# A transformer block on one core: the closing sums are dealt to VectorE, TensorE and GpSimd by a table, two parts more are read ahead, and the reads begin at another signal

## The chip, the cores and the metric

One core of a Trainium2 chip runs the whole program. The metric is the time on the device in microseconds (us), the median of several executions. Engines are called PE or TensorE (matmuls), DVE or VectorE, ACT or ScalarE, POOL or GpSimd; SP only issues DMAs.

## The reference, cut to what matters

The input is 64 sequences of 64 tokens of 256 floats (4096 tokens). A conditioned down/up projection, attention and a routed feed-forward layer follow. The end of it is what the change touches: each token goes to 4 of 32 experts, and their weighted outputs are added to the token's residual and to the input.

```python
topv, topi = jax.lax.top_k(glogits, TOPK)            # TOPK = 4 of E = 32
gw = jax.nn.softmax(topv, axis=-1)
combine = jnp.zeros((N, E), x.dtype).at[jnp.arange(N)[:, None], topi].add(gw)
def body(acc, we):
    wu, wd, ce = we
    u, g = (h2 @ wu)[:, :DFF], (h2 @ wu)[:, DFF:]
    return acc + ce[:, None] * (jax.nn.silu(g) * u @ wd), None
y2, _ = jax.lax.scan(body, jnp.zeros_like(h2), (W_up, W_down, combine.T))
return x + y2.reshape(Bx, Tx, Dx)                    # and the caller: x = x + this
```

## The kernel before

The first part (to about 575 us) computes attention and routing and writes each token's row into lists in DRAM, one list for each expert. The second part, the expert loop, walks over `NET` = 161 tiles of 128 list rows. The number is the worst case; how many tiles hold rows is known only at run time, and here 142 do (the last 19 are empty and are computed all the same). For each tile ACT starts the load of its rows (`rows_in`, six tiles ahead), PE turns and multiplies them with the expert's weights, which lie in a ring of four slots, DVE and ACT do the elementwise work, ACT writes the result to `rows_out` (`NY` = 6 buffers), and POOL scatters it by an indirect DMA to `pick_rows` in DRAM, where the four results of a token lie side by side (`s_put`, six semaphores, one for each buffer, count the landings). Every twelve tiles DVE also adds input rows into `resid`, which holds the residual of all tokens in SBUF.

The end follows the loop in each engine's program. `PARTS` = 8 parts of `NP` = 4 token tiles are read back from `pick_rows`, 2 MB each (`picks`: for a tile of 128 tokens, 4 rows of 256 floats on each partition). SP issues the reads into `NPICK` = 5 buffers: part 5 goes into the buffer of part 0 and so on, so it waits until part 0's sums are done. SP issues the first read when `s_rows_out` has reached the number of filled tiles plus 6; the tile that brings it there could only be written after the last filled tile's scatter had landed, because it uses the same buffer.

Of each part DVE sums three tiles in three instructions: first the four rows of each tile to two, then the two to one, then into `resid`. PE sums the fourth by matmuls with the identity into PSUM (one for `resid`, four for the picks), and ACT copies that from PSUM into `resid` and issues the tile's store. Ahead of its first copy ACT waits for the last six scatters to land. SP stores DVE's three tiles of each part, after it has issued all reads.

Each engine runs its own program in order; the order of the first part stands in hand-written tables and is not touched.

Of the kernel before, what the change touches and what calls it, by code (L numbers as in the profile page):

```python
# [23 lines left out]
E, TOPK, DFF = 32, 4, 256  # L24
# [7 lines left out]
NT = NTOK // P  # L32
# [16 lines left out]
WE = KC * 2 * DFF + FC * D  # L49
# [5 lines left out]
NW, NU, NPAY, NG, NY, NC = 5, 3, 3, 10, 6, 4  # L55
# [4 lines left out]

NP = 4
PARTS = NT // NP
NPICK = 5
BATCH = 8

NX, XSTEP = 4, 12

# [152 lines left out]
def program(nc, d):  # L220
# [30 lines left out]
    def sb1(name, shape, dt=F32):  # L251
# [175 lines left out]
    s_sum, s_summed = sem("s_sum"), sem("s_summed")  # L427
    s_act_upper, s_up_upper, s_up_split = sem("s_act_upper"), sem("s_up_upper"), sem("s_up_split")


# [48 lines left out]
    def sync_program(e):  # L479
# [108 lines left out]
        w.wait_ge(s_ug, 1)  # L588
        for k in range(2 * TPM):
            w.wait_ge(s_x2_row[(LAST - k) % (2 * TPM)], 16 * ((LAST - k) // (2 * TPM) + 1))  # L590
        e.dma_start(resid[:, :, :], x2_rows.rearrange("(t p) n -> p t n", p=P)).then_inc(s_back, 16)
        w.wait_ge(s_ring_wait, 1)
        for n in range(RING, E):
# [4 lines left out]

        w.wait_ge(s_resid, NT // NX)
# [9 lines left out]
        for c in range(PARTS):  # L611
            w.wait_ge(s_final, c + 1)
            e.dma_start(d["out"][c * NP * P:(c * NP + NP - 1) * P, :].rearrange("(t p) n -> p t n", p=P),
                        resid[:, c * NP:c * NP + NP - 1, :]).then_inc(s_out, 16)
        w.wait_ge(s_out, 16 * 2 * PARTS)

    def gpsimd_program(e):
# [78 lines left out]

        for i in range(NET):
            scatter(i)  # L700

    def tensor_program(e):
# [317 lines left out]


        w.wait_ge(s_mid, NET)
        for c in range(PARTS):
            bank, t = gbank[c % 2][:, 0:D], c * NP + NP - 1
            if c >= 2:
                w.wait_ge(s_summed, c - 1)
            w.wait_ge(s_resid, NT // NX)
            e.matmul(bank, ident[:, :], resid[:, t, :], start=True, stop=False)  # L1030
            w.wait_ge(s_picks[c % NPICK], 16 * (c // NPICK + 1))
            for k in range(TOPK):
                ins = e.matmul(bank, ident[:, :], picks[c % NPICK][:, NP - 1, k, :], start=False, stop=k == TOPK - 1)
            ins.then_inc(s_sum, 1)

    def scalar_program(e):
# [244 lines left out]
        for c in range(PARTS):  # L1283
            t = c * NP + NP - 1
            w.wait_ge(s_sum, c + 1)
            e.activation(resid[:, t, :], gbank[c % 2][:, 0:D], ACT.Copy).then_inc(s_summed, 1)
            w.wait_ge(s_summed, c + 1)
            e.dma_start(d["out"][t * P:(t + 1) * P, :], resid[:, t, :]).then_inc(s_out, 16)

    def vector_program(e):
# [334 lines left out]
        e.tensor_scalar(all_out[:, :], ends[0:1, E - 1:E], float(AHEAD + NY), None, ALU.add)  # L1627
# [24 lines left out]
        def turn_mid(i):  # L1652
# [15 lines left out]
        for i in range(NET + 2):  # L1668
            if i >= 2:
                turn_mid(i - 2)  # L1670
            if 0 < i < NET - 2:
                turn_in(i + 2)
            if i < NET:
                expert_mid(i)
            if i == 0:
                turn_in(2)
            if i % XSTEP == 0 and 3 <= i // XSTEP < 3 + NT // NX:
                residual(i // XSTEP - 3)

        for c in range(PARTS):  # L1680
            pk = picks[c % NPICK]
            w.wait_ge(s_picks[c % NPICK], 16 * (c // NPICK + 1))
            at = slice(c * NP, c * NP + NP - 1)
            half = own.mark(e.tensor_tensor(pk[:, 0:NP - 1, 0:2, :], pk[:, 0:NP - 1, 0:2, :], pk[:, 0:NP - 1, 2:4, :], ALU.add))
            w.wait_ge(s_vector, half)
            whole = own.mark(e.tensor_tensor(pk[:, 0:NP - 1, 0, :], pk[:, 0:NP - 1, 0, :], pk[:, 0:NP - 1, 1, :], ALU.add))
            w.wait_ge(s_back, 16)
            w.wait_ge(s_vector, whole)
            e.tensor_tensor(resid[:, at, :], resid[:, at, :], pk[:, 0:NP - 1, 0, :], ALU.add).then_inc(s_final, 1)

    banks_for = banks_of()
    with ctx:
# [23 lines left out]
def _constants():  # L1716

    f = np.float32
    p = np.arange(P)
    pos = np.arange(T, dtype=f) / f(32.0)  # L1720
    inv = (f(1.0) / np.power(f(150000.0), np.arange(0, DH, 2, dtype=f) / f(DH))).astype(f)
    angle = (pos[:, None] * inv[None, :]).astype(f)
    cos, sin = np.cos(angle).T[p % 32], np.sin(angle).T[p % 32]
    scale = f(DH ** -0.5)

    unused = np.zeros((P, ROW), f)
    unused[:, D] = PAIRS + p
# [19 lines left out]


# [48 lines left out]
```

## Time and profile before

| what | value |
|---|---|
| median of 3 runs | 1031.28 us (1029.86 to 1033.35) |
| profiled execution, first to last instruction (its span) | 1031.5 us |
| busy share of the span: PE, DVE, ACT, POOL | 87%, 78%, 50%, 54% |
| bytes moved by DMA | 251.95 MB, mean 244 GB/s |

The profiled execution is one execution; the record gives its span, and no other time of it, and the span is 0.2 us above the median of the runs. Times in the trace are counted from the span's start. Busy shares are means over stages that have different limits, so the end must be read by itself. The loop's last DVE instruction ends at 996 us, and everything after that is the end.

### The profile page before, as it was taken

Reading aid. Unit: us, or ns where it says so; the run is one execution under the profiler, and the core shown is the slowest. Engines: PE = TensorE matmul, PEld = TensorE weight load, DVE = VectorE, ACT = ScalarE, POOL = GpSimd, SP = SyncE. Lnnn points to the kernel's source line nnn. Section 1 sums busy time; section 2 is a strip of 40 time slices with the busy share of each in tenths; the row PEclk is TensorE's granted clock in tenths of the full one; section 3 lists DMA queues with packets and bytes.
Section 4 is the critical chain, followed back from the end, with each engine's and each line's share of the span. In section 5 each row is a group of like instructions: output and inputs, shape, how many; then the busy total and the mean of one; then the engine's idle time right before and its main releaser. Section 6 shows DMA issues by size and latency. Waiting matters only on the chain.

```text
span 1031.5 us, 21542 instructions
## 1 busy us (share of the span) xinstructions
PE 898.5 (87%) x7336; PEld 738.7 (72%) x7336; DVE 805.3 (78%) x1877; ACT 512.2 (50%) x1193; POOL 552.1 (54%) x513
## 2 busy tenths in 40 slices
PE   3859998988899989988871399999999999999986
PEld 1537676776677767766750288888888888888874
DVE  3878799988978898988857177777777777777787
ACT  1224362735437363453752266666666666566631
POOL 2436466877768688696768133333433344333340
PEclk9869999999999999999995599999999999999998
DMA  7235869687696977959875897778678758663599
GB/s 224 57 93 181 268 218 268 224 275 250 232 290 214 295 241 252 293 192 301 289 252 202 325 307 266 264 243 309 224 254 273 265 186 308 223 226 103 179 365 340
DMA packets 127684, 251.95 MB, mean 244 GB/s; under 512 B 18706, under 2 KB 66327, under 8 KB 127002
## 3 DMA queue, kind: packets, MB, share of 16 engines
q1 hardware_dynamic: 83866, 187.59, 55.4%
q0 software_dynamic: 13872, 34.64, 9.2%
q10 hardware_dynamic: 29840, 28.34, 9.0%
q8 instruction: 63, 1.03, 0.4%
q14 instruction: 43, 0.35, 0.1%
HBM read 136.19 MB, written 102.66 MB: 232 GB/s over the span
## 4 chain that ended last, share of the span: by engine, by line
PE 49%; POOL 14%; DMA 11%; DVE 10%; issue 7%; SPq 4%; ACT 3%; ACTq 0%; DVEq 0%; POOLq 0%
PE scores L970 10%; PE gbank L970 10%; POOL lists L672 10%; PE scores L989 5%; PE gbank L989 5%; DMA w_parts<-ring 4%; PE gbank L761 3%; DMA ring<-in_W_up 3%; POOL ring L679 3%; PE gbank L838 3%; DMA rows_in<-lists 3%; DVE ring L1401 2%; PE gbank L944 2%; PE scores L944 2%; PE gbank L979 2%
## 5 line engine op out<-in xcount | busy, mean ns | idle before, releaser
L694 POOL DMA_INDIRECT pick_rows<-rows_out,pair_i x161 | 160.9, 999 | 269.4 <-ACT rows_out L1232 260.7
L679 POOL TENSOR_TENSOR ring<-ring 128x512 fp32r<-128x512 f32 x96 | 122.6, 1291 | 47.0 <-ACT ring L1167 46.5
L970 PE MATMUL scores<-ring,in_part 128*128 x486 | 134.7, 412 | 0.0
L970 PE MATMUL gbank<-ring,in_part 128*128 x480 | 131.8, 409 | 0.0
L672 POOL DMA_INDIRECT lists<-put_rows,slot_i x104 | 103.4, 994 | 47.5 <-issue 28.0
L838 PE MATMUL gbank<-w_o,ring 128*128 128x256 f32 x512 | 123.2, 396 | 6.0 <-ACT ring L1113 6.0
L761 PE MATMUL gbank<-h_t,w_qk 128*128 128x512 f32 x480 | 122.1, 407 | 6.7 <-DVE h_t L1388 5.0
L1401 DVE SCALAR_TENSOR_TENSOR ring<-gbank,b_qk,rope 128x512 f32<-128x512 f32 x160 | 109.9, 745 | 16.6 <-PE gbank L761 16.0
L838 PEld LDWEIGHTS gbank<-w_o,ring 128*128 128x128 f32 x512 | 99.8, 199 | 26.0 <-ACT ring L1113 9.7
L761 PEld LDWEIGHTS gbank<-h_t,w_qk 128*128 128x128 f32 x480 | 89.7, 192 | 31.5 <-issue 8.6
L1167 ACT ACTIVATE ring<-ring 128x512 fp32r<-128x512 f32 x96 | 59.9, 628 | 90.8 <-DMA w_parts<-ring 50.9
L970 PEld LDWEIGHTS scores<-ring,in_part 128*128 128x128 f32 x486 | 86.1, 191 | 15.0
L970 PEld LDWEIGHTS gbank<-ring,in_part 128*128 128x128 f32 x480 | 84.3, 189 | 14.5
L1218 ACT ACTIVATE in_part<-scores,norm_w 128x128 fp32r<-128x128 f32 x162 | 50.8, 365 | 51.3 <-PE scores L944 33.7
L989 PEld LDWEIGHTS gbank<-ring,mid_part 128*128 128x128 f32 x486 | 67.6, 188 | 7.7 <-issue 0.4
L989 PEld LDWEIGHTS scores<-ring,mid_part 128*128 128x128 f32 x480 | 66.8, 188 | 7.2
L989 PE MATMUL gbank<-ring,mid_part 128*128 x486 | 69.2, 278 | 0.1
L989 PE MATMUL scores<-ring,mid_part 128*128 x480 | 68.2, 278 | 0.0
L1648 DVE SCALAR_TENSOR_TENSOR mid<-scores,rows_in,silu 128x256 f32<-128x256 f32 x81 | 39.1, 483 | 35.7 <-ACT silu L1224 35.7
L1224 ACT ACTIVATE silu<-scores,rows_in 128x256 f32<-128x256 f32 x81 | 38.6, 477 | 51.2 <-PE scores L970 51.2
L1638 DVE TENSOR_TENSOR pair_i<-rows_in,twice 128x1 int32<-128x1 f32 x161 | 25.7, 160 | 48.8 <-ACT in_part L1218 39.6
L1105 ACT ACTIVATE ring<-gbank 128x512 f32<-128x512 f32 x64 | 34.5, 588 | 55.0 <-PE gbank L812 55.0
(200 smaller groups left out, 1899.0 us busy)
## 6 DMA issues: line engine op xcount, KB each, us to landing
w_parts<-ring SPq DMA_DIRECT2D x192, 256.0 KB, 3.2
ring<-w_parts SPq DMA_DIRECT2D x32, 1536.0 KB, 7.9
rows_in<-lists ACTq DMA_DIRECT2D x161, 136.0 KB, 3.8
ring<-in_W_up SPq DMA_DIRECT2D x64, 256.0 KB, 4.0
picks<-pick_rows SPq DMA_DIRECT2D x8, 2048.0 KB, 12.8
ring<-in_W_down SPq DMA_DIRECT2D x32, 256.0 KB, 4.2
q_r<-rot SPq DMA_DIRECT2D x16, 512.0 KB, 6.9
q_r<-ring SPq DMA_DIRECT2D x16, 512.0 KB
```

Of the source, the lines that this page charges most:

```text
L672: e.indirect_dma_start(out=lists, out_offset=bass.IndirectOffsetOnAxis(ap=slot_i[r % NPAY][:, s * TOPK + k:s * TOPK + k + 1], axis=0), in_ ...
L679: e.tensor_tensor(lower, lower.bitcast(F32), upper.bitcast(F32), ALU.subtract).then_inc(s_lower, 1)
L694: e.indirect_dma_start(out=pick_rows, out_offset=bass.IndirectOffsetOnAxis(ap=pair_i[:, i:i + 1], axis=0), in_=rows_out[i % NY][:, :], in_ ...
L761: ins = e.matmul(bank[:, :], w_qk[:, x, c, 2 * j + o, :], h_t[i][:, y, c, :], start=k == 0, stop=k == len(CHUNK_PRODUCTS) - 1)
L838: e.matmul(bank[:, 0:D], y_t[:, n // REP, n % REP, :, :].rearrange("p b s -> p (b s)"), w_o[:, n, :], start=n == 0, stop=False)
L944: ins = e.transpose(bank[:, c * P:(c + 1) * P], rows_in[i % NG][:, c * P:(c + 1) * P], ident[:, :])
L970: ins = e.matmul(front[i % FRONTS], in_parts[i % IN_BUFS][x][:, c, :], ring[:, bass.ds(at + y * WE + c * 2 * DFF, 2 * DFF)], start=k == 0, ...
L989: ins = e.matmul(out, mid_parts[i % 2][x][:, c, :], ring[:, bass.ds(at + y * WE + KC * 2 * DFF + c * D, D)], start=k == 0, stop=k == len(C ...
L1167: e.activation(w_upper[q % NU], w_third[q % NW].bitcast(F32), ACT.Copy).then_inc(s_upper, 1)
L1218: ins = e.activation(in_parts[i % IN_BUFS][0][:, c, :], front[i % FRONTS][:, c * P:(c + 1) * P], ACT.Copy, scale=norm2_w[:, c:c + 1])
L1401: e.scalar_tensor_tensor(out=by_seq(t[n][:, :]), in0=by_seq(gbank[banks[o]][:, :]), scalar=b_qk[:, 2 * j + o:2 * j + o + 1], in1=rope[:, t ...
L1648: e.scalar_tensor_tensor(out=mid[i % MID_BUFS][:, :], in0=front[i % FRONTS][:, 0:DFF], scalar=rows_in[i % NG][:, D + 2:D + 3], in1=silu[i ...
```

## The change

`NPICK` grows to 7: parts 5 and 6 get buffers in ring slots 0 to 2 (the last expert's weights are in slot 3). A table `SUMS` says for each part how many tiles go to DVE, PE and POOL; over the eight parts DVE gets 17 of 32 tiles (24 before), PE 10 (8 before) and POOL 5 (none before). POOL does its sums with the same three adds, after its last scatter. The first read waits on the six `s_put` semaphores for exactly the landings of the filled tiles; DVE works those counts out once in the loop (`put_waits`, three small instructions, after tile 12), and SP loads them. ACT no longer waits for the last scatters; POOL does, at its end. One small table (`put_no`) is loaded, and `plan_wait` is held in 16 bits in place of 32.

```diff
-NPICK = 5
+NPICK = 7
+SUMS = [(3, 1, 0), (3, 1, 0), (1, 2, 1), (2, 1, 1), (2, 1, 1), (1, 2, 1), (2, 1, 1), (3, 1, 0)]
...
-    picks = [first] + [sb(f"picks{i}", [P, NP, TOPK, D]) for i in range(1, NPICK)]
+    picks = [first] + [sb(f"picks{i}", [P, NP, TOPK, D]) for i in range(1, NPICK - 2)]
+    picks += [ring_space[:, i * NP * TOPK * D:(i + 1) * NP * TOPK * D].rearrange("p (t k n) -> p t k n", t=NP, k=TOPK)
+              for i in range(2)]
...
+    by_tensor = [(c, n + k) for c, (n, by_pe, _) in enumerate(SUMS) for k in range(by_pe)]
+    thirds = [sum(by_pool for _, _, by_pool in SUMS[:c + 1]) for c in range(PARTS)]
...  SP
-        rows = e.value_load(all_out[0:1, 0:1], min_val=NY + 1, max_val=NET + NY)
-        e.wait_ge(s_rows_out, rows)
+        for k in range(NY):
+            e.wait_ge(s_put[k], puts[k])
...  SP, in the loops over parts
-                w.wait_ge(s_sum, c - NPICK + 1)
+                w.wait_ge(s_tile_sum, sum(p <= c - NPICK for p, _ in by_tensor))
+                w.wait_ge(s_third_sum, thirds[c - NPICK])
...
+            if SUMS[c][2]:
+                t = c * NP + NP - 1
+                w.wait_ge(s_third_sum, thirds[c])
+                e.dma_start(d["out"][t * P:(t + 1) * P, :], resid[:, t, :]).then_inc(s_out, 16)
...  POOL, after its last scatter
+        for c in range(PARTS):
+            if SUMS[c][2]:
+                pk, t = picks[c % NPICK], NP - 1
+                w.wait_ge(s_picks[c % NPICK], 16 * (c // NPICK + 1))
+                w.wait_ge(s_resid, NT // NX)
+                e.tensor_tensor(pk[:, t, 0:2, :], pk[:, t, 0:2, :], pk[:, t, 2:4, :], ALU.add).then_inc(s_third_half, 1)
+                w.wait_ge(s_third_half, thirds[c])
+                e.tensor_tensor(pk[:, t, 0, :], pk[:, t, 0, :], pk[:, t, 1, :], ALU.add).then_inc(s_third_whole, 1)
+                w.wait_ge(s_third_whole, thirds[c])
+                e.tensor_tensor(resid[:, c * NP + t, :], resid[:, c * NP + t, :], pk[:, t, 0, :], ALU.add).then_inc(
+                    s_third_sum, 1)
...  ACT
-        for k in range(NY):
-            w.wait_ge(s_put[(NET - 1 - k) % NY], 16 * ((NET - 1 - k) // NY + 1))
-        e.sem_inc(s_rows_out, NY)
...  DVE, in the loop after tile 12
+            below = own.mark(e.tensor_scalar(put_tiles[:, :, :], put_no[:, :, :], ends[0:1, E - 1:E], 16.0, ALU.is_lt,
+                                             ALU.mult))
+            below = own.mark(e.tensor_reduce(put_count[:, :], put_tiles[:, :, :], axis=AX.X, op=ALU.add))
+            e.tensor_copy(put_wait[:, :], put_count[:, :]).then_inc(s_put_wait, 1)
```

On DVE, in the closing sums, these are the rows of parts 2 and 3 before (a name with its buffer's number, the shape of the result or of what is read, and the semaphore waited for).

```order
L1684 TENSOR_TENSOR picks2<-picks2 128x3x512 [waits s_picks2]
L1686 TENSOR_TENSOR picks2<-picks2 128x3x256 [waits s_vector]
L1689 TENSOR_TENSOR resid<-resid,picks2 128x768 [waits s_vector]
L1684 TENSOR_TENSOR picks3<-picks3 128x3x512 [waits s_picks3]
L1686 TENSOR_TENSOR picks3<-picks3 128x3x256 [waits s_vector]
L1689 TENSOR_TENSOR resid<-resid,picks3 128x768 [waits s_vector]
```

And these are the same two parts on DVE after the change.

```order
L1730 TENSOR_TENSOR picks2<-picks2 128x512 [waits s_picks2]
L1732 TENSOR_TENSOR picks2<-picks2 128x256 [waits s_vector]
L1735 TENSOR_TENSOR resid<-resid,picks2 128x256 [waits s_vector]
L1730 TENSOR_TENSOR picks3<-picks3 128x2x512 [waits s_picks3]
L1732 TENSOR_TENSOR picks3<-picks3 128x2x256 [waits s_vector]
L1735 TENSOR_TENSOR resid<-resid,picks3 128x512 [waits s_vector]
```

The number of DVE's instructions is the same, 24, and each is as long as its part's tiles: one tile in parts 2 and 5, two in 3, 4 and 6, three in 0, 1 and 7.

POOL's program ended, before, with its last scatters and a branch.

```order
L694 DMA pick_rows<-rows_out2,pair_i 16384x256 [waits s_rows_out]
L694 DMA pick_rows<-rows_out3,pair_i 16384x256 [waits s_rows_out]
L694 DMA pick_rows<-rows_out4,pair_i 16384x256 [waits s_rows_out]
L1692 UNCONDITIONAL_BRANCH
```

After the change the sums of five tiles follow on POOL; the first two of them:

```order
L719 DMA pick_rows<-rows_out4,pair_i 16384x256 [waits s_rows_out]
L732 TENSOR_TENSOR picks2<-picks2 128x512 [waits s_resid,s_picks2]
L734 TENSOR_TENSOR picks2<-picks2 128x256 [waits s_third_half]
L736 TENSOR_TENSOR resid<-resid,picks2 128x256 [waits s_third_whole]
L732 TENSOR_TENSOR picks3<-picks3 128x512 [waits s_picks3]
L734 TENSOR_TENSOR picks3<-picks3 128x256 [waits s_third_half]
L736 TENSOR_TENSOR resid<-resid,picks3 128x256 [waits s_third_whole]
```

POOL thus has 15 instructions of its own in the end, and both operands of each lie in SBUF, as DVE's do.

## Rows read from the trace of the kernel before

**Rows 1.** Stretches: busy us of PE, PEld, DVE, ACT, POOL; PE clock, DMA share, GB/s.

```profile
970.00:996.00 26.00, 25.86 (x166) 22.96 (x164) 18.89 (x58) 14.52 (x36) 10.51 (x11) 1.00 1.02 381
...
1025.40:1029.00 3.60, 0.00 (x0) 0.00 (x0) 0.00 (x0) 0.00 (x0) 0.00 (x0) 0.96 1.09 385
```

**Rows 2.** Chain that ended last: start us, length us, what (first and last of 24).

```profile
996.05 1.68 DVE picks L1684
...
1024.43 0.96 DVE resid L1689
```

**Rows 3.** DVE's groups from 996 us: count, busy us, mean ns, idle before.

```profile
L1684 DVE TENSOR_TENSOR picks<-picks 128x1536 f32<-128x1536 f32 x8 | 14.0, 1752 | 0.0
L1686 DVE TENSOR_TENSOR picks<-picks 128x768 f32<-128x768 f32 x8 | 7.7, 958 | 0.3
L1689 DVE TENSOR_TENSOR resid<-resid,picks 128x768 f32<-128x768 f32 x8 | 7.7, 958 | 0.3
```

**Rows 4.** Timeline of PE in the end: first matmuls of three tiles.

```profile
997.00 0.59 PE L1030 MATMUL gbank<-resid,ident 128*128 128x256 f32 x2
...
1016.07 0.59 PE L1030 MATMUL gbank<-resid,ident 128*128 128x256 f32 x2
...
1018.23 0.59 PE L1030 MATMUL gbank<-resid,ident 128*128 128x256 f32 x2
```

**Rows 5.** Waits from 996 us: who waited for what, us, times, longest.

```profile
ACT resid L1286 <- DMA pick_rows<-rows_out,pair_i: 9.2, 1, 9.2
```

**Rows 6.** Timeline of POOL and SP: last filled tile's scatter, first read.

```profile
955.17 0.98 POOL L694 DMA_INDIRECT pick_rows<-rows_out,pair_i  x1 [1.55 <-ACT rows_out L1232]
...
969.60 0.36 SPq L608 DMA_DIRECT2D picks<-pick_rows  x1
```

**Rows 7.** Source view of the fifth read alone: issue ns, start us, landing.

```profile
L608 SPq DMA_DIRECT2D picks<-pick_rows x1: 6727/6727/6727, 975.3 to 975.3; - x1
...
DMA to landing us min/median/max: 26.2/26.2/26.2
```

**Rows 8.** Timeline, DVE's first sums beside POOL's last scatters.

```profile
995.97 1.75 DVE L1684 TENSOR_TENSOR picks<-picks 128x1536 f32<-128x1536 f32 x1
996.62 1.95 POOL L694 DMA_INDIRECT pick_rows<-rows_out,pair_i  x1 [0.30 <-issue]
...
999.62 1.75 DVE L1684 TENSOR_TENSOR picks<-picks 128x1536 f32<-128x1536 f32 x1
...
1000.86 1.36 POOL L694 DMA_INDIRECT pick_rows<-rows_out,pair_i  x1 [0.30 <-issue]
```

**Rows 9.** Timeline of the first part: adds on POOL beside comparisons on DVE, twice.

```profile
211.62 1.31 POOL L663 TENSOR_TENSOR rot<-ring 128x512 f32<-128x512 f32 x1
211.81 1.66 DVE L1472 TENSOR_TENSOR onehot<-expert_no,top_f 128x512 f32<-128x512 f32 x1
...
514.32 0.69 DVE L1472 TENSOR_TENSOR onehot<-expert_no,top_f 128x512 f32<-128x512 f32 x1
514.32 1.82 POOL L679 TENSOR_TENSOR ring<-ring 128x512 fp32r<-128x512 f32 x1 [1.47 <-ACT ring L1167]
```

**Rows 10.** POOL's groups over the span: an add and a memset.

```profile
L679 POOL TENSOR_TENSOR ring<-ring 128x512 fp32r<-128x512 f32 x96 | 122.6, 1291 | 47.0 <-ACT ring L1167 46.5
...
L622 POOL MEMSET ones<- 128x128 f32 x1 | 0.2, 202 | 0.0
```

**Rows 11.** Source view of SP's last store, 384 KB: issue ns, start us, landing.

```profile
L613 SPq DMA_DIRECT2D out<-resid x1: 372/372/372, 1025.4 to 1025.4; - x1
...
DMA to landing us min/median/max: 5.7/5.7/5.7
```

**Rows 12.** Source view of line 491, 128 KB stores of the first part: landings.

```profile
DMA to landing us min/median/max: 2.6/3.7/7.2
```

**Rows 13.** Row loads issued from 970 to 981 us, beside the reads: landings.

```profile
DMA to landing us min/median/max: 6.3/6.9/7.1
```

**Rows 14.** Timeline of PE at the loop's last wait for a row load.

```profile
885.59 0.44 PE L944 MATMUL scores<-ident,rows_in 128*128 128x128 f32 x2 [0.77 <-DMA rows_in<-lists]
```

More of the change, by code:

```diff
@@ L10 @@
 F32, I32, U32, BF16 = mybir.dt.float32, mybir.dt.int32, mybir.dt.uint32, mybir.dt.bfloat16
+U16 = mybir.dt.uint16
 F32R = mybir.dt.float32r
@@ L366, in program @@
     plan_slot = sb("plan_slot", [1, 2 * P], I32)
-    plan_wait = sb("plan_wait", [1, 2 * P], I32)
+    plan_wait = sb("plan_wait", [1, 2 * P], U16)
     ring_wait = sb("ring_wait", [1, E], I32)
-    all_out = sb("all_out", [1, 1], I32)
+    put_no = sb("put_no", [1, NY, PUTS])
+    put_tiles = sb("put_tiles", [1, NY, PUTS])
+    put_count = sb("put_count", [1, NY])
+    put_wait = sb("put_wait", [1, NY], I32)
     rows_in = [sb(f"rows_in{i}", [P, ROW]) for i in range(NG)]
@@ L426, in program @@
         sem(f"s_{n}") for n in ("expert", "ring_wait", "plan", "in_lower", "mid", "mid_parts", "final"))
-    s_sum, s_summed = sem("s_sum"), sem("s_summed")
+    s_summed, s_tile_sum, s_put_no, s_put_wait = (
+        sem(f"s_{n}") for n in ("summed", "tile_sum", "put_no", "put_wait"))
+    s_third_half, s_third_whole, s_third_sum = (sem(f"s_third_{n}") for n in ("half", "whole", "sum"))
     s_act_upper, s_up_upper, s_up_split = sem("s_act_upper"), sem("s_up_upper"), sem("s_up_split")
@@ L597, in sync_program @@
             say_ready(n)
+        w.wait_ge(s_put_wait, 1)
+        _, puts = nc.values_load_multi_w_load_instructions(
+            put_wait[0:1, 0:NY], engines=[mybir.EngineType.SP], min_val=16, max_val=16 * PUTS)
         w.wait_ge(s_resid, NT // NX)
-        rows = e.value_load(all_out[0:1, 0:1], min_val=NY + 1, max_val=NET + NY)
-        e.wait_ge(s_rows_out, rows)
+        for k in range(NY):
+            e.wait_ge(s_put[k], puts[k])
         for c in range(PARTS):
@@ L611, in sync_program @@
         for c in range(PARTS):
+            n = SUMS[c][0]
             w.wait_ge(s_final, c + 1)
-            e.dma_start(d["out"][c * NP * P:(c * NP + NP - 1) * P, :].rearrange("(t p) n -> p t n", p=P),
-                        resid[:, c * NP:c * NP + NP - 1, :]).then_inc(s_out, 16)
-        w.wait_ge(s_out, 16 * 2 * PARTS)
+            e.dma_start(d["out"][c * NP * P:(c * NP + n) * P, :].rearrange("(t p) n -> p t n", p=P),
+                        resid[:, c * NP:c * NP + n, :]).then_inc(s_out, 16)
+            if SUMS[c][2]:
+                t = c * NP + NP - 1
+                w.wait_ge(s_third_sum, thirds[c])
+                e.dma_start(d["out"][t * P:(t + 1) * P, :], resid[:, t, :]).then_inc(s_out, 16)
+        w.wait_ge(s_out, 16 * sum(1 + by_pe + by_pool for _, by_pe, by_pool in SUMS))
     def gpsimd_program(e):
@@ L700, in gpsimd_program @@
             scatter(i)
+        for c in range(PARTS):
[9 more added lines that the diff above has]
+                    s_third_sum, 1)
+        for k in range(NY):
+            w.wait_ge(s_put[(NET - 1 - k) % NY], 16 * ((NET - 1 - k) // NY + 1))
     def tensor_program(e):
@@ L1024, in tensor_program @@
         w.wait_ge(s_mid, NET)
[L1025 to L1028, printed above, removed]
+        for n, (c, t) in enumerate(by_tensor):
+            bank = gbank[n % 2][:, 0:D]
+            if n >= 2:
+                w.wait_ge(s_summed, n - 1)
             w.wait_ge(s_resid, NT // NX)
-            e.matmul(bank, ident[:, :], resid[:, t, :], start=True, stop=False)
+            e.matmul(bank, ident[:, :], resid[:, c * NP + t, :], start=True, stop=False)
             w.wait_ge(s_picks[c % NPICK], 16 * (c // NPICK + 1))
             for k in range(TOPK):
-                ins = e.matmul(bank, ident[:, :], picks[c % NPICK][:, NP - 1, k, :], start=False, stop=k == TOPK - 1)
-            ins.then_inc(s_sum, 1)
+                ins = e.matmul(bank, ident[:, :], picks[c % NPICK][:, t, k, :], start=False, stop=k == TOPK - 1)
+            ins.then_inc(s_tile_sum, 1)
     def scalar_program(e):
@@ L1278, in scalar_program @@
                 load_x_rows(i // XSTEP - 2)
-        for k in range(NY):
-            w.wait_ge(s_put[(NET - 1 - k) % NY], 16 * ((NET - 1 - k) // NY + 1))
-        e.sem_inc(s_rows_out, NY)
[L1283 to L1288, printed above, removed]
+        for n, (c, t) in enumerate(by_tensor):
+            w.wait_ge(s_tile_sum, n + 1)
+            e.activation(resid[:, c * NP + t, :], gbank[n % 2][:, 0:D], ACT.Copy).then_inc(s_summed, 1)
+            w.wait_ge(s_summed, n + 1)
+            e.dma_start(d["out"][(c * NP + t) * P:(c * NP + t + 1) * P, :], resid[:, c * NP + t, :]).then_inc(s_out, 16)
     def vector_program(e):
@@ L1658, in turn_mid, with put_waits @@
             e.tensor_tensor(lower[:, :, :], turned, upper[:, :, :].bitcast(F32), ALU.subtract).then_inc(s_mid_parts, 1)
+        def put_waits():
+            w.wait_ge(s_put_no, 16)
+            below = own.mark(e.tensor_scalar(put_tiles[:, :, :], put_no[:, :, :], ends[0:1, E - 1:E], 16.0, ALU.is_lt,
+                                             ALU.mult))
+            w.wait_ge(s_vector, below)
+            below = own.mark(e.tensor_reduce(put_count[:, :], put_tiles[:, :, :], axis=AX.X, op=ALU.add))
+            w.wait_ge(s_vector, below)
+            e.tensor_copy(put_wait[:, :], put_count[:, :]).then_inc(s_put_wait, 1)
         def residual(c):
@@ L1678, in vector_program @@
                 residual(i // XSTEP - 3)
+            if i == XSTEP:
+                put_waits()
         for c in range(PARTS):
@@ L1682, in vector_program @@
             w.wait_ge(s_picks[c % NPICK], 16 * (c // NPICK + 1))
-            at = slice(c * NP, c * NP + NP - 1)
-            half = own.mark(e.tensor_tensor(pk[:, 0:NP - 1, 0:2, :], pk[:, 0:NP - 1, 0:2, :], pk[:, 0:NP - 1, 2:4, :], ALU.add))
+            n = SUMS[c][0]
+            at = slice(c * NP, c * NP + n)
+            half = own.mark(e.tensor_tensor(pk[:, 0:n, 0:2, :], pk[:, 0:n, 0:2, :], pk[:, 0:n, 2:4, :], ALU.add))
             w.wait_ge(s_vector, half)
-            whole = own.mark(e.tensor_tensor(pk[:, 0:NP - 1, 0, :], pk[:, 0:NP - 1, 0, :], pk[:, 0:NP - 1, 1, :], ALU.add))
+            whole = own.mark(e.tensor_tensor(pk[:, 0:n, 0, :], pk[:, 0:n, 0, :], pk[:, 0:n, 1, :], ALU.add))
             w.wait_ge(s_back, 16)
             w.wait_ge(s_vector, whole)
-            e.tensor_tensor(resid[:, at, :], resid[:, at, :], pk[:, 0:NP - 1, 0, :], ALU.add).then_inc(s_final, 1)
+            e.tensor_tensor(resid[:, at, :], resid[:, at, :], pk[:, 0:n, 0, :], ALU.add).then_inc(s_final, 1)
     banks_for = banks_of()
@@ L1745, in _constants @@
         "fill_rows": unused,
+        "put_no": (np.arange(NY)[:, None] + NY * np.arange(PUTS)[None, :] - AHEAD)[None].astype(f),
     }
```

4 lines of the change are left out of this document (3 added, 1 removed).

## The prediction

> **What bounds the kernel now.** The views by stretch come first. While the first five parts are read (970 to 996 us) PE is busy 25.86 of 26.00 us at a granted clock of 1.00, and the DMA engines are full at 381 GB/s [rows 1]. So the loop is PE's, and nothing that this change does there can shorten it. The chain that ended last shows what comes after: from 996.05 us to 1025.39 (1024.43 + 0.96) it is DVE's sums, 24 instructions end to end [rows 2]. The groups give 1.752 us for the first instruction of a part and 0.958 for each of the two others, with at most 0.3 us idle in all [rows 3]; 8 x 3.67 = 29.4 us is the whole stretch. PE needs 1018.23 - 1016.07 = 2.16 us for a tile [rows 4], 17 us for its eight, and is held up once because ACT waits 9.2 us for the last scatters [rows 5], but it is not what ends last. After DVE's last sum comes SP's last store, which lands 5.7 us after its issue at 1025.4 [rows 11], that is at 1031.1; the span ends 0.4 us later, at 1031.5. All of these numbers are of that one execution; the median of the runs is 0.2 us less.
>
> So the reader should see two terms that set the end: the time of the sums from 996 us, and the tail of the last store.
>
> **Reads that start earlier, two parts more.** The last filled tile's scatter is issued at 955.17 and takes 0.98 us to issue [rows 6]; with about 2 us to land the reads could begin at 958, not at 969.6, some 11.5 us earlier. The fifth read landed at 975.3 + 26.2 = 1001.5 [rows 7]. One part is 2 MB, 5.5 us at 381 GB/s, so seven parts from 958 us end at 1001.5 - 11.5 + 2 x 5.5 = 1001. DVE did not wait for a read before, so this is worth nothing by itself. Part 7 goes into part 0's buffer and needs part 0's sums (999.7) to be done; even with 26.2 us it lands when the sums reach it. I count zero.
>
> **The sums, if the three engines worked side by side.** From 1.752 and 0.958 for 1536 and 768 elements [rows 3], DVE costs 1.034 ns an element and 0.16 us an instruction. A part of three tiles takes 3.67 us, of two 1.22 + 0.69 + 0.69 = 2.61, of one 0.69 + 0.43 + 0.43 = 1.55. The table gives 3 x 3.67 + 3 x 2.61 + 2 x 1.55 = 21.9 us, so DVE would end at 1017.9. PE has ten tiles of 2.16 us from 997.0 [rows 4]: 1018.6. ACT's wait is gone, so nothing holds PE up.
>
> **What GpSimd's five tiles cost DVE.** This decides. All of DVE's sums and all of GpSimd's read two operands in SBUF. The trace has such pairs in the first part, and they do not overlap. At 211.81 DVE's comparison of 512 elements begins, 0.2 us after an add on GpSimd, and takes 1.66 us in place of 0.69; it ends 0.54 us after GpSimd's end (211.62 + 1.31 = 212.93), which is its 512 elements at 1.034 ns. At 514.32 both begin together, DVE takes its 0.69 us, and GpSimd takes 1.82, ending 1.13 us after DVE [rows 9]; undisturbed its mean is 1.29 [rows 10]. So whichever comes second waits for the whole of the other, and only its start, about 0.15 us, is hidden. In the end itself the last scatters show that GpSimd is let in where one of DVE's instructions ends: they last 1.95 and 1.36 us and end 0.85 us after DVE's ends at 997.72 and 1001.37 [rows 8]. I take it that they alternate.
>
> The Trainium skill says the same in "SBUF — State Buffer", section "Who interferes with whom": an instruction of VectorE with two inputs in SBUF contends with a GpSimd instruction that reads SBUF, and whoever issues second is blocked to the other's end. By that rule the sums of the two engines add up and end at 1027.2; without it they end at 1017.9. The two pairs in the trace agree with the rule, with the 1.66 and 1.82 us above.
>
> Until 1002.37 the program is as before (parts 0 and 1 keep three tiles on DVE, and GpSimd's last scatter ends at 1000.86 + 1.36 = 1002.22). What then remains must pass one at a time:
> - DVE: part 1's last add (768 elements) and 11 tiles of 1024, 12,032 x 1.034 ns = 12.4 us.
> - GpSimd: 15 adds. One of 512 elements holds the other engine 1.13 us. One of 256 is not in the trace: not below half of that, 0.57, and not above 1.13. A memset of 128 columns takes 0.20 us in all [rows 10], so little of an instruction is fixed, and I take 0.58. Five tiles of 1.13 + 2 x 0.58: 11.5 us.
> - GpSimd's 15 instructions run out before DVE's 19; DVE's last four or five pay their start again, about 0.2 us each: 0.9 us.
>
> Sum: 1002.4 + 12.4 + 11.5 + 0.9 = 1027.2, against 1025.4 before: **1.8 us later**. What DVE gives up (7 tiles, 7.4 us) and the hidden starts (about 2.2 us) are less than what GpSimd takes.
>
> **The tail.** Before, SP issued its stores only after its last read, which waited for sums on PE, and the DMA engines still ran at 385 GB/s from 1025.4 to 1029.0 with nothing but stores left [rows 1]; the last store stood behind that. After, SP has issued all reads at about 1000, stores go out as sums are done, and the last one finds the engines empty. A store of 128 KB landed in 2.6 us at best, 3.7 in the median [rows 12]; 384 KB is 256 KB more, 0.7 us at 385 GB/s. I take 3.3 in place of 5.7: **2.4 us earlier**; bounds 2.6 and 5.7.
>
> **The small edits.** DVE's three instructions after tile 12 work on one partition; DVE is idle 27% of a stretch of the loop (18.89 of 26.00 busy [rows 1]), PE has work queued, and each costs under 0.4 us: zero, at most 1 us without that cover. The six register loads on SP come long before the reads. The 16-bit table and the removed addition I count at nothing: each is one instruction of 256 elements or fewer. Reads that begin earlier run beside more of the loop: a tile takes about 2.5 us there (26 us for some ten tiles), row loads are issued four tiles, 10 us, ahead of PE's use, and beside reads they land in 6.3 to 7.1 us [rows 13], so the loop holds.
>
> **Sum:** 1031.5 + 1.8 - 2.4 = 1030.9 in the profile's terms, 0.2 less as a median: **1030.7 us**, no change that can be told. I take 0.3% (3.1 us) as what a measurement of this kernel can tell.
>
> **Rivals.**
> - *Side by side* (chance 0.15): the exclusion does not bind these adds. GpSimd would need 5 x (1.29 + 2 x 0.74) = 13.9 us from 1002.2, 1016.1; DVE ends at 1017.9, PE at 1018.6, ACT's copy and store add 0.4 and 3.3, the span's end 0.4: 1022.7, as a median 1022.5. For it: GpSimd's adds and DVE's sums mostly touch different buffers, and two pairs are few. Against: in both pairs the later one waited to the end of the other [rows 9].
> - *GpSimd's short adds do not shrink* (chance 0.17): if 256 elements hold DVE as long as 512, ten of them cost 0.55 us more each, the sums end at 1032.7 and the time is 1036. It decides from about 0.3 us more each: 0.88 us gives 1033.7, and with a tail of 3.7 and 0.4 lost at hand-overs 1034.4, slower by 0.3%. For it: no row has so short an add on GpSimd. Against: the memset.
> - *The loop stalls* (chance 0.06): seven reads beside the loop delay row loads or scatters. Once in the loop PE waited 0.77 us for a row load [rows 14], with other transfers beside it. A tile's worth of it, 2 to 5 us, gives 1033 to 1036. Against: at 381 GB/s PE kept 25.86 of 26.00 us busy.
> - *The end does not move* (part of the forecast): if the last store is as slow as before, 5.7 us, the time is 1033.1, still within the bound.
>
> **How the numbers follow.** The forecast, sums that alternate and a shorter tail, has 0.62; its own range is 1028.5 to 1033.5. Side by side has 0.15, the long adds 0.17, the stall 0.06. Faster by over 0.3% comes from side by side, and 0.03 of the forecast where the hand-over hides more than 0.15 us: 0.18. Slower comes from most of the long adds and of the stall: 0.21. The same: 0.61. The range leaves out side by side (0.15) and the worst of the long adds: 1027 to 1035.
>
> **What the profile will show.** Right: the closing sums on DVE are stretched from about 1002 on (a 1024-element instruction at 1.7 to 2.3 us, with GpSimd's adds between), GpSimd ends near 1022, DVE near 1027, PE is done by 1019 and idle at the end, the first read is issued at 958, and the last store lands in 3 to 4 us. Wrong: DVE's instructions keep 1.22 and 0.69 us beside GpSimd's adds, or GpSimd's adds of 256 elements take over 1 us by themselves, or the loop's last tile comes later than 996.

## The result, and the profile after

The changed kernel takes 1041.24 us (median of 6 runs, 1038.47 to 1049.84) where the kernel before took 1032.93 beside it (6 runs): ratio 1.0091, 95% interval 1.0067 to 1.0116. It is slower by 0.9%, outside the range. The profiled execution is the slowest of the six (span 1048.0 us, 16.5 more than that of before); its shape counts here, its size by the ratios. One execution of `e14_pad160` below (3413.41 us, where its nine others took 1030.62 to 1035.10) counts in no ratio.

The end is what the prediction was about, and there it holds. In the timeline of VectorE and GpSimd after (start us, length us, engine, line):

```profile
1013.74 1.75 DVE L1730 TENSOR_TENSOR picks<-picks 128x1536 f32<-128x1536 f32 x1
...
1025.34 0.79 POOL L734 TENSOR_TENSOR picks<-picks 128x256 f32<-128x256 f32 x1
1025.46 1.74 DVE L1730 TENSOR_TENSOR picks<-picks 128x1024 f32<-128x1024 f32 x1
1026.20 1.58 POOL L736 TENSOR_TENSOR resid<-resid,picks 128x256 f32<-128x256 f32 x1
...
1027.75 1.71 POOL L732 TENSOR_TENSOR picks<-picks 128x512 f32<-128x512 f32 x1
1028.37 1.64 DVE L1735 TENSOR_TENSOR resid<-resid,picks 128x512 f32<-128x512 f32 x1
...
1044.10 0.96 DVE L1735 TENSOR_TENSOR resid<-resid,picks 128x768 f32<-128x768 f32 x1
```

VectorE's sums run from 1013.74 to 1045.06, 31.3 us in place of 29.4 [rows 2, 3]. Instructions of the two engines now hold each other up: VectorE's 512 elements take up to 1.64 us beside GpSimd, 1024 take 1.74, while GpSimd's 256 take 0.79 where they come first and up to 1.58 where they come second. The source view of SP's store line after 1045 us answers to [rows 11]:

```profile
L634 SPq DMA_DIRECT2D out<-resid x1: 383/383/383, 1045.1 to 1045.1; - x1
...
DMA to landing us min/median/max: 2.5/2.5/2.5
```

It lands in 2.5 us, not 5.7. From VectorE's first sum to the span's end it is 34.3 us, and was 35.5 (996.05 to 1031.5): the end has become shorter by 1.2 us. What grew is the loop: its last VectorE instruction ended at 996, and ends at 1013.8. The first and the 121st and 141st tile, as ACT writes them, after:

```profile
596.87 0.47 ACT L1271 ACTIVATE rows_out<-gbank,rows_in 128x256 f32<-128x256 f32 x1 [0.24 <-PE gbank L1028]
...
915.68 0.47 ACT L1271 ACTIVATE rows_out<-gbank,rows_in 128x256 f32<-128x256 f32 x1 [0.24 <-PE gbank L1028]
...
966.88 0.47 ACT L1271 ACTIVATE rows_out<-gbank,rows_in 128x256 f32<-128x256 f32 x1 [0.24 <-PE gbank L1028]
```

and before:

```profile
595.76 0.47 ACT L1232 ACTIVATE rows_out<-gbank,rows_in 128x256 f32<-128x256 f32 x1 [0.21 <-PE gbank L989]
...
900.80 0.47 ACT L1232 ACTIVATE rows_out<-gbank,rows_in 128x256 f32<-128x256 f32 x1 [0.21 <-PE gbank L989]
...
951.39 0.47 ACT L1232 ACTIVATE rows_out<-gbank,rows_in 128x256 f32<-128x256 f32 x1 [0.21 <-PE gbank L989]
```

The reader sees two things. Twenty undisturbed tiles take 51.20 us in place of 50.59, 2.560 each in place of 2.529. And 120 tiles up to there took 318.8 us in place of 305.0: more than 120 x 0.03, so there are stalls too. The waits of PE between 600 and 1010 us name them (total us, times, longest):

```profile
PE gbank L1028 <- issue: 5.1, 6, 1.1
...
PE scores L983 <- DMA rows_in<-lists: 2.6, 4, 1.1
...
PE gbank L983 <- DMA rows_in<-lists: 1.7, 2, 1.3
```

Before, the row loads cost PE 1.0 us in all, and there was no wait of the first kind ("issue": the profile shows nothing that PE waited for). One of those, in PE's timeline, and below it the source view of line 996 in the same stretch (the load of eight values of `plan_wait` into PE's registers, once in eight tiles):

```profile
707.31 0.44 PE L983 MATMUL scores<-ident,rows_in 128*128 128x128 f32 x2 [1.06 <-DMA rows_in<-lists]
707.50 1.65 PE L1009 MATMUL gbank<-ring,in_part 128*128 x6
710.23 0.98 PE L1028 MATMUL gbank<-ring,mid_part 128*128 x6 [1.08 <-issue]
```

```profile
L996 PEldq TENSOR_LOAD <-plan_wait x1: 2267/2267/2267, 707.8 to 707.8; - x1
```

The load runs from 707.8 to 710.1, and the matmul that stands behind it starts at 710.23, after 1.08 us without work. Over the whole span (ns, shortest, median and longest of 21), after and then before:

```profile
L996 PEldq TENSOR_LOAD <-plan_wait x21: 1922/2011/2387, 565.1 to 1004.0; - x21
```

```profile
L957 PEldq TENSOR_LOAD <-plan_wait x21: 587/592/792, 565.1 to 986.8; - x21
```

Held in 16 bits, the same eight values take 2.0 us to load in place of 0.59.

### The profile page after: what moved, and what is told of

Same layout as the page of the kernel before. It is cut to its first block, busy times and chain, and to the rows that moved or that the text cites. A ratio compares the mean times of both kernels' runs of the same rounds, so it can differ in the third digit from the quotient of the medians.

```text
span 1048.0 us, 21590 instructions
## 1 busy us (share of the span) xinstructions
PE 909.2 (87%) x7324; PEld 747.8 (71%) x7356; DVE 813.1 (78%) x1879; ACT 511.9 (49%) x1195; POOL 570.3 (54%) x528
## 4 chain that ended last, share of the span: by engine, by line
PE 48%; POOL 14%; DMA 12%; DVE 11%; issue 8%; ACT 4%; SPq 3%; ACTq 1%; DVEq 0%; POOLq 0%
POOL lists L697 10%; PE gbank L1009 9%; PE scores L1009 9%; DMA rows_in<-lists 6%; PE gbank L1028 5%; PE scores L1028 5%; PE gbank L800 4%; PE gbank L877 4%; DMA w_parts<-ring 3%; POOL ring L704 3%; DVE ring L1436 2%; PE scores L983 2%; DMA ring<-in_W_up 2%; PE gbank L983 1%; PE gbank L1018 1%
## 5 line engine op out<-in xcount | busy, mean ns | idle before, releaser
L800 PEld LDWEIGHTS gbank<-h_t,w_qk 128*128 128x128 f32 x480 | 90.0, 192 | 31.3 <-issue 8.6
L1028 PE MATMUL gbank<-ring,mid_part 128*128 x486 | 72.6, 285 | 5.3 <-issue 5.1
L1257 ACT ACTIVATE in_part<-scores,norm_w 128x128 fp32r<-128x128 f32 x162 | 50.6, 363 | 53.2 <-PE scores L983 35.5
L1028 PE MATMUL scores<-ring,mid_part 128*128 x480 | 70.4, 282 | 0.0
```

Of the source, the lines that this page charges most:

```text
L800: ins = e.matmul(bank[:, :], w_qk[:, x, c, 2 * j + o, :], h_t[i][:, y, c, :], start=k == 0, stop=k == len(CHUNK_PRODUCTS) - 1)
L1028: ins = e.matmul(out, mid_parts[i % 2][x][:, c, :], ring[:, bass.ds(at + y * WE + KC * 2 * DFF + c * D, D)], start=k == 0, stop=k == len(C ...
L1257: ins = e.activation(in_parts[i % IN_BUFS][0][:, c, :], front[i % FRONTS][:, c * P:(c + 1) * P], ACT.Copy, scale=norm2_w[:, c:c + 1])
```

## The experiments

**Theory A:** the loss is two things that the change does to the loop without meaning to. The narrow table makes PE's register loads 1.4 us longer; and the new small tables (with `plan_wait` halved) moved every buffer that is placed behind them in SBUF, `rows_in`, `in_part`, `mid`, `mid_part` and more, by 864 bytes, after which each tile of the loop takes 0.03 us longer. **Theory B:** the earlier reads delay the loop's row loads. **Theory C:** GpSimd's sums cost the 0.9%.

### The load and the placement, apart and together

`e1_wait32` is the changed kernel with the table at 32 bits (the mask is an operation on a register and leaves the values, 1 to 32, as they are):

```diff
-    plan_wait = sb("plan_wait", [1, 2 * P], U16)
+    plan_wait = sb("plan_wait", [1, 2 * P], I32)
...
-                slot_of[i] = (slots[i // BATCH][i % BATCH], readies[i // BATCH][i % BATCH])
+                slot_of[i] = (slots[i // BATCH][i % BATCH], readies[i // BATCH][i % BATCH] & 63)
```

> The changed kernel with plan_wait held in 32 bits again, and each value masked with 63 on TensorE's sequencer before it is waited for (the mask is in this run's kernel alone and in those that say so). Theory A, narrow load and placement: TensorE's load of eight 16-bit values takes 2.0 us where the 32-bit one took 0.59, and the loop's tiles moved by 864 bytes to addresses that are 32 above a multiple of 64, which costs 0.026 us a tile. By A the load goes back to about 0.6 us, the tiles stay at 2.556 us, and the kernel is about 6 us faster than the change: ratio to before 1.003. Theory B, the reads that begin earlier hold up row loads: the load's time changes, but the kernel stays at 1.009. Theory C, the closing sums on GpSimd cost the time: stays at 1.009.

`e2_align` leaves the table at 16 bits and puts 32 bytes of padding ahead of the moved tiles:

```diff
     put_wait = sb("put_wait", [1, NY], I32)
+    shift = sb("shift", [P, 8])
```

> The changed kernel with 32 unused bytes ahead of rows_in, so that all tiles of the loop lie at multiples of 64 again; plan_wait stays at 16 bits. By A the tile goes back to 2.53 us in undisturbed stretches, 161 x 0.026 = 4.2 us, and the load stays at 2.0 us: ratio to before about 1.005. By B and C nothing changes: 1.009.

`e3_both` has both edits.

> The changed kernel with both undone (32-bit plan_wait with the mask, 32 bytes ahead of rows_in). By A only the end differs from before: the sums end about 1.9 us later after the loop, the last store lands about 3 us sooner after them: ratio to before 0.999, and the sums still alternate between VectorE and GpSimd. By B or C: 1.009.

`e5_before_u16` is the kernel before with the narrow table alone:

```diff
-    plan_wait = sb("plan_wait", [1, 2 * P], I32)
+    plan_wait = sb("plan_wait", [1, 2 * P], mybir.dt.uint16)
```

> The kernel before, with plan_wait held in 16 bits and nothing else changed (tiles stay at multiples of 64). By A TensorE's load takes 2.0 us in place of 0.59 and stalls of about 1 us show in some of the 21 batches: 4 to 8 us slower than before, ratio 1.004 to 1.008. By B and C: no change.

Measured, 12 runs each beside the kernel before (1034.35 us in that set):

| kernel | median us | ratio, 95% interval | first to 141st tile in the trace, us |
|---|---|---|---|
| `e1_wait32` (load undone) | 1035.31 | 1.0010 (0.9996 to 1.0023) | 594.83 to 956.82: 362.0 |
| `e2_align` (placement undone) | 1039.15 | 1.0038 (1.0019 to 1.0056) | 593.52 to 957.27: 363.8 |
| `e3_both` (both undone) | 1032.14 | 0.9972 (0.9952 to 0.9992) | 596.49 to 952.12: 355.6 |
| `e5_before_u16` (narrow load alone) | 1040.05 | 1.0053 (1.0032 to 1.0075) | 594.57 to 955.47: 360.9 |

By the rows above the same stretch takes 370.0 us in the changed kernel and 355.6 before: with both undone the loop is as long as it was.

The source view of the register load in `e1_wait32`:

```profile
L996 PEldq TENSOR_LOAD <-plan_wait x21: 587/590/897, 564.5 to 994.4; - x21
```

and in `e5_before_u16`, with its stall in the waits:

```profile
L957 PEldq TENSOR_LOAD <-plan_wait x21: 1927/2038/2407, 562.4 to 991.0; - x21
```

```profile
PE gbank L989 <- issue: 2.5, 3, 1.0
```

The width alone sets the load's time, in either kernel, and the wait "issue" comes and goes with it: `e1_wait32` and `e3_both` have none. Tiles 121 and 141 of `e3_both` are 50.50 us apart, 2.525 each:

```profile
901.62 0.48 ACT L1272 ACTIVATE rows_out<-gbank,rows_in 128x256 f32<-128x256 f32 x1 [0.24 <-PE gbank L1029]
...
952.12 0.47 ACT L1272 ACTIVATE rows_out<-gbank,rows_in 128x256 f32<-128x256 f32 x1 [0.24 <-PE gbank L1029]
```

where `e1_wait32`, the same program with its buffers 32 bytes lower, has 2.560:

```profile
905.62 0.47 ACT L1271 ACTIVATE rows_out<-gbank,rows_in 128x256 f32<-128x256 f32 x1 [0.24 <-PE gbank L1028]
...
956.82 0.47 ACT L1271 ACTIVATE rows_out<-gbank,rows_in 128x256 f32<-128x256 f32 x1 [0.24 <-PE gbank L1028]
```

Theory A stands, and B and C fall as the cause of the loss: `e3_both` keeps early reads and GpSimd's sums, and is not slower than the kernel before. Against B speaks the order in time too. In the changed kernel PE's last wait for a row load up to 1010 us comes long before the first read:

```profile
878.17 0.44 PE L983 MATMUL scores<-ident,rows_in 128*128 128x128 f32 x2 [0.49 <-DMA rows_in<-lists]
...
974.72 11.38 SPq L628 DMA_DIRECT2D picks<-pick_rows  x5
```

The load costs 0.0053 to 0.0081 (1.0091 - 1.0010, 1.0038 - 0.9972, `e5_before_u16`), 5.5 to 8.4 us; the placement 0.0038 to 0.0053 (the other two differences), 4 to 5.5 us, where 161 x 0.035 is 5.6. In `e1_wait32` the load is dearer than A expected (1.003 expected, 1.0010 measured), in `e5_before_u16` it is within what A expected.

### Which placement is slow

`e4_before_shift` puts the padding into the kernel before (and the mask of `e1_wait32`):

```diff
+    shift = sb("shift", [P, 8])
     rows_in = [sb(f"rows_in{i}", [P, ROW]) for i in range(NG)]
```

> The kernel before with 32 bytes of padding ahead of the tiles that the change also moved (so they stand at 32 mod 64 bytes, as after the change), the table left at 32 bits; the register's value is masked once for each tile. Theory of placement: every undisturbed tile takes 2.556 us in place of 2.530, 161 x 0.026 = 4.2 us, ratio 1.004. Rival: it is another part of the change that slowed the tiles by 0.026 us (and the padding in the other experiments undid it by chance): tiles at 2.530 us, ratio 1.000.

Its tiles take 2.546 us (tiles 121 and 141 at 897.36 and 948.27), 0.017 more than before: the placement alone slows this kernel too, by two thirds of what was expected (0.026). The ratio, 1.0010 (0.9989 to 1.0031), cannot tell 161 x 0.017 = 2.7 us from nothing. So I tried other paddings in `e3_both`:

```diff
-    shift = sb("shift", [P, 8])
+    shift = sb("shift", [P, 24])    e11_pad96
+    shift = sb("shift", [P, 16])    e12_pad64
+    shift = sb("shift", [P, 32])    e13_pad128
+    shift = sb("shift", [P, 40])    e14_pad160
```

> The kernel of e3_both with 96 bytes of padding in place of 32: the moved tiles stand 960 bytes behind their places in the kernel before, again at 0 mod 64. Theory that the remainder to 64 bytes decides: tiles at 2.520 to 2.53 us as in e3_both, ratio 0.997. Rival, something else in the addresses decides and 32 bytes hit it by chance: tiles at 2.54 to 2.56 us, ratio near 1.001.

> The kernel of e3_both with 64 bytes of padding in place of 32: 928 bytes behind, at 32 mod 64 as in e1_wait32. Theory that the remainder to 64 bytes decides: tiles at 2.545 to 2.56 us, ratio near 1.001. Rival, something else in the addresses: tiles at 2.52 to 2.53 us, ratio 0.997.

> The kernel of e3_both with 128 bytes of padding in place of 32: rows_in's first buffer at byte 95,264, a remainder of 32 to 128 bytes, as in the changed kernel and in e1_wait32 (remainder 32: 2.553 to 2.560 us a tile). Theory that the remainder to 128 bytes decides (64: 2.525 to 2.529 us so far; 0: 2.543; 96: 2.538 to 2.546; 32: the slowest): 2.553 to 2.560 us a tile, ratio 1.000 to 1.001. Rival, the fit to 128 bytes is an accident of six placements: a tile takes 2.52 to 2.545 us.

> The kernel of e3_both with 160 bytes of padding in place of 32: rows_in's first buffer at byte 95,296, a remainder of 64 to 128 bytes, as in the kernel before and in e3_both. Theory that the remainder to 128 bytes decides: 2.525 to 2.530 us a tile, ratio 0.997. Rival, the fit is an accident: 2.535 us or more, ratio 0.999 or more.

Addresses, in the table, are those of the first `in_part` buffer in the built programs, as the remainder to 256 bytes:

| remainder | kernels | us a tile, tiles 121 to 141 | ratio |
|---|---|---|---|
| 32 | after, `e1_wait32` | 2.560, 2.560 | 1.0091, 1.0010 |
| 64 | `e2_align`, `e3_both` | 2.525, 2.525 | 1.0038, 0.9972 |
| 96 | `e12_pad64` | 2.538 | 0.9999 (0.9976 to 1.0023) |
| 128 | `e11_pad96` | 2.543 | 0.9995 (0.9974 to 1.0016) |
| 160 | `e13_pad128` | 2.543 | 1.0015 (0.9991 to 1.0040) |
| 192 | before, `e5_before_u16`, `e14_pad160` | 2.529, 2.529, 2.529 | 1, 1.0053, 0.9979 (0.9960 to 0.9997) |
| 224 | `e4_before_shift` | 2.546 | 1.0010 |

The rows of `e13_pad128`, which decided against a rule by 128 bytes (50.87 us for twenty tiles, where 51.06 to 51.20 was expected):

```profile
905.40 0.48 ACT L1272 ACTIVATE rows_out<-gbank,rows_in 128x256 f32<-128x256 f32 x1 [0.24 <-PE gbank L1029]
...
956.27 0.47 ACT L1272 ACTIVATE rows_out<-gbank,rows_in 128x256 f32<-128x256 f32 x1 [0.24 <-PE gbank L1029]
```

The remainder to 64 bytes falls with `e11_pad96` (2.543 us where 2.520 to 2.53 was expected; `e12_pad64`, 2.538, fits neither side of its expectation), that to 128 with `e13_pad128` (`e14_pad160` alone came as it said). The remainder to 256 agrees with all placements, and gives the same time in the three programs at 192; but that was read off afterwards.

PE's groups over these twenty tiles show in which instructions the time lies: those of `e1_wait32`, then of `e3_both`, then of the kernel before (busy us, mean ns; as many again write to `gbank`, with the same busy times and means).

```profile
L1009 PE MATMUL scores<-ring,in_part 128*128 x60 | 16.5, 410 | 0.0
L1028 PE MATMUL scores<-ring,mid_part 128*128 x60 | 8.8, 282 | 0.0
```

```profile
L1010 PE MATMUL scores<-ring,in_part 128*128 x60 | 16.2, 406 | 0.0
L1029 PE MATMUL scores<-ring,mid_part 128*128 x60 | 8.7, 280 | 0.0
```

```profile
L970 PE MATMUL scores<-ring,in_part 128*128 x60 | 16.5, 409 | 0.0
L989 PE MATMUL scores<-ring,mid_part 128*128 x60 | 8.5, 277 | 0.0
```

Between `e1_wait32` and `e3_both` most of the 0.70 us lies in the matmuls that read `in_part` (2 x 0.3). The kernel before has nearly the time of `e3_both` in another way: its `in_part` matmuls are as slow as those of `e1_wait32`, and its `mid_part` matmuls are the fastest of the three. `e14_pad160`, at the same remainder as before, has the same two means (409 and 277 ns). VectorE's and ACT's instructions that write `in_part` keep their means (343 and 344 ns, 363 and 365 in `e1_wait32` and `e3_both`). That the placement sets the tile's time, by up to 0.035 us, and that the time lies in PE's matmuls, is shown; by which rule, and by the address of which of the moved buffers, stays open.

### GpSimd's share, and the early reads

`e6_no_pool` is `e3_both` with GpSimd's sums given to VectorE (there are five of them, not four as the expectation says; VectorE has 17 tiles in `e3_both` and 22 here), and `e9_twelve` gives two more to TensorE:

```diff
-SUMS = [(3, 1, 0), (3, 1, 0), (1, 2, 1), (2, 1, 1), (2, 1, 1), (1, 2, 1), (2, 1, 1), (3, 1, 0)]
+SUMS = [(3, 1, 0), (3, 1, 0), (2, 2, 0), (3, 1, 0), (3, 1, 0), (2, 2, 0), (3, 1, 0), (3, 1, 0)]
...  e9_twelve, e9_again
+SUMS = [(3, 1, 0), (2, 2, 0), (3, 1, 0), (2, 2, 0), (3, 1, 0), (2, 2, 0), (2, 2, 0), (3, 1, 0)]
```

> The kernel of e3_both with GpSimd's four sums given away: two to VectorE (parts 3, 4, 6 and others then hold three of VectorE's tiles) and two parts with two tiles of TensorE, so VectorE 22 tiles, TensorE 10, GpSimd none. Theory of exclusion (VectorE and GpSimd hold each other up while both have two inputs in SBUF): VectorE alone takes 3.67 us for a part of three tiles and 2.61 for one of two, 6 x 3.67 + 2 x 2.61 = 27.2 us in place of 31.3, TensorE's ten tiles end 3 to 4 us before that, so the end comes 4.1 us earlier than in e3_both: ratio to the kernel before 0.993 where e3_both had 0.997. Rival, side by side: GpSimd's sums cost VectorE nothing, its four tiles come on top of VectorE's 31.3 us, 4 x 1.06 us: 4 us later than e3_both, ratio 1.001.

> As e6_no_pool, with two more tiles from VectorE to TensorE: VectorE 20, TensorE 12, GpSimd none. VectorE 4 x 3.67 + 4 x 2.61 = 25.1 us; TensorE's tiles came every 2.16 us in e3_both from 998.5 on, with its loop's last VectorE instruction at 997.0: 12 of them end 27.4 us after that point, with 0.4 us of eviction behind them. So TensorE becomes the bound: end within 1 us of e6_no_pool, ratio 0.993. Rival: where VectorE and not TensorE were still last, the end would come 2.1 us before that of e6_no_pool, ratio 0.991.

The timeline of VectorE in `e6_no_pool`, first and last sum:

```profile
995.43 1.75 DVE L1731 TENSOR_TENSOR picks<-picks 128x1536 f32<-128x1536 f32 x1
...
1021.65 0.96 DVE L1736 TENSOR_TENSOR resid<-resid,picks 128x768 f32<-128x768 f32 x1
```

With five tiles more VectorE is done in 27.2 us, not 31.3: 1028.09 us, ratio 0.9932 (0.9910 to 0.9953). Exclusion is right to the tenth, side by side falls. In `e9_twelve` VectorE's sums end at 1019.8, and ACT's last copy and store for TensorE come later:

```profile
1021.87 0.38 ACT L1322 ACTIVATE resid<-gbank 128x256 f32<-128x256 f32 x1 [1.77 <-PE gbank L1073]
1022.28 0.34 ACTq L1324 DMA_DIRECT2D out<-resid  x1
```

1026.18 us, ratio 0.9913 (0.9892 to 0.9935): TensorE is now the bound. The ratio is that of the rival, the mechanism that of the theory: from VectorE's first sum to the span's end it is 30.2 us in `e6_no_pool` and 29.7 here, less by 0.5 and not by 2.1, and the intervals of the two ratios overlap.

`e8_late_reads` and `e10_twelve_late` hold the reads until the old time, in `e3_both` and in `e9_twelve` (run again as `e9_again`):

```diff
+        e.wait_ge(s_rows_out, 148)
         for c in range(PARTS):
```

> The kernel of e3_both with one more wait ahead of the reads: for the count of filled tiles at which the kernel before let them begin (142 tiles). My theory: where the reads begin is worth nothing, ratio 0.997 as e3_both, tile after tile at the same 2.53 us. Rival one, early reads slow the loop (they share queues with the row loads): 1 to 4 us faster than e3_both, 0.994 to 0.996. Rival two, early reads are what lets the sums run without waiting: VectorE waits for parts, ratio 1.000 or more.

> The kernel of e9_twelve once more, word for word, as the other side of e10_twelve_late in the same set of runs: ratio to the kernel before 0.991 again, 25.1 us of VectorE's sums, the last store from ScalarE's side some 2.1 us before the end.

> The kernel of e9_again with reads held until 142 tiles are filled, as in the kernel before (e8_late_reads did this to e3_both, whose TensorE then waited 1.9 us for a part's rows at no cost, since VectorE ended last). My theory: the loop does not feel where the reads begin, but here TensorE's sums end last, and they now wait about 1.9 us: 0 to 2 us slower than e9_again, ratio 0.991 to 0.993. Rival: early reads slow the loop by 2.5 us (the difference of e8_late_reads and e3_both in two separate sets of runs): 1 to 2.5 us faster than e9_again, 0.989 to 0.990.

`e8_late_reads`: 1029.35 us, 0.9947 (0.9928 to 0.9966), first read at 968.38 and not 958.51. That is the ratio of rival one, but not its mechanism: in the profiled executions it is 402.3 us from the first tile to VectorE's first sum (592.80 to 995.14), and 400.5 in `e3_both` (596.49 to 996.99), so the loop was not faster; the end is 34.3 us in both. The 0.0025 between two sets of runs has no place in the stretches that the edit touches, and the intervals overlap. `e9_again`: 1026.65 us, 0.9934 (0.9912 to 0.9956), not the 0.991 of its first set. `e10_twelve_late`: 1029.98 us, 0.9957 (0.9938 to 0.9975), slower by 0.0023, though the intervals overlap. That is near the 0 to 2 us of my theory, but not by its mechanism: TensorE's last store is issued at the same time in both (1025.38, 1025.35). The stretches of `e9_again` from 1015 and 1020 us (columns as in [rows 1]):

```profile
1015.00:1020.00 5.00, 5.00 (x25) 4.41 (x24) 4.86 (x7) 0.77 (x2) 0.00 (x0) 1.00 0.59 201
1020.00:1025.00 5.00, 4.93 (x23) 4.00 (x21) 2.83 (x3) 0.80 (x3) 0.00 (x0) 1.00 0.48 170
```

and of `e10_twelve_late`:

```profile
1015.00:1020.00 5.00, 5.00 (x25) 4.39 (x24) 4.07 (x6) 0.77 (x2) 0.00 (x0) 1.00 1.05 399
1020.00:1025.00 5.00, 4.90 (x23) 3.98 (x21) 3.67 (x3) 0.83 (x3) 0.00 (x0) 1.00 1.09 381
```

With late reads the DMA engines are full to the end: VectorE waits 1.1 us for the last part, SP's stores from 1015 us on land in 6.5 us in the median where they took 2.5, and the end grows from 29.7 to 31.2 us.

## Why the prediction was wrong

**The step that failed** is in the small edits: "The 16-bit table and the removed addition I count at nothing: each is one instruction of 256 elements or fewer." It priced the instruction that writes the table, and not the 21 that read it on PE. The loads grow by 1.42 us each, 30 us in all; `e5_before_u16` gives 5.5 us for this alone, so most of the 30 is hidden and the rest stops the loop. Six of the 21 loads show in PE's waits after the change. Four of these waits (ending at 710.23, 795.14, 817.46 and 880.75 us) come within 3 us of a wait for a row load, after which PE can have had little queued; two (901.87 and 985.09) do not, and what exposes those is open.

**A term was missing**: the new tables moved the loop's buffers, and the placement costs 4 to 5.5 us. The prediction has no such term: it weighs a longer loop only for VectorE's three instructions and for the reads ("so the loop holds", and the rival "the loop stalls" with 0.06). The loop did get longer, but `e3_both` rules out the reads as the cause.

**What held.** With both undone the change is worth 0.9972 (0.9952 to 0.9992), somewhat better than the forecast for the rest (1030.7 against 1031.28 us, 0.9994) and at the lower edge of the forecast's own range (1028.5 us, 0.9973). The traces show 1.2 us of it in the end (34.3 against 35.5 us); for the rest they show no place.
- *The sums*: +1.8 us forecast, +1.9 measured; GpSimd ends 5 us before VectorE, as said. A short add that waits ends 0.58 us after VectorE's instruction (1026.20 + 1.58 against 1025.46 + 1.74), as I took, and lengthens an instruction of 1024 elements by 0.52 us (1.74 against 1.22); the rival of long adds falls with that. The rule of the Trainium skill ("SBUF — State Buffer", section "Who interferes with whom"), by which the one issued second is blocked to the other's end, agrees with these rows and with the 27.2 us of `e6_no_pool`.
- *The tail*: 3.7 us forecast from the last store's issue to the span's end, 2.9 measured. The 384 KB store landed in 2.5 us, so the 0.7 us added for its size were wrong.
- *Early reads*: zero, right for this table. In `e3_both` the first read is at 958.51 (forecast 958). Once the sums are shorter, the traces show 1.5 us for them (29.7 against 31.2 us).
- *`put_waits`*: `e3_both` contains it, and its first 140 tiles take the 355.6 us of before; no cost is seen.

## What to carry to other kernels

When a change makes a table narrower or adds a small buffer, ask who reads the table, and on which engine's sequencer, and which buffers have moved: neither shows in the order of instructions. Check the time of one undisturbed tile, and the register loads, before looking at the part that was meant to change. And work dealt to a second engine that holds up the first while it runs is no gain: once the two accidents are undone, the tables without GpSimd's sums give the fastest kernels here (0.9932, and 0.9913 and 0.9934 with twelve tiles on TensorE).

## What was not expected of the hardware

- A register load of eight values takes 0.59 us at 32 bits each and 2.0 us at 16 bits, though it moves half the bytes.
- The address of the loop's buffers within SBUF changes a tile of the loop from 2.525 to 2.560 us, with the same instructions in the same order, and the time lies mostly in PE's matmuls that read `in_part` and `mid_part` (means of 406 to 410 and 277 to 282 ns). It repeats to 0.002 us at equal remainders to 256 bytes.
- Row loads cost PE between 0.7 and 4.3 us of waits from 600 us on in the profiled executions of these kernels, and also differ between kernels with equal placement and register loads (0.8 in `e3_both`, 2.4 in `e8_late_reads`); why is open.
